# A first chunk prepared its own way: early statistics, own banks, and the spread of the deviations moved from memory to TensorE

## The chip, the cores and the metric

The kernel runs on one core of a Trainium2 chip. The time is that of the device, in microseconds, from the first to the last instruction of the core with what lies around them; lower is better. TensorE multiplies matrices into PSUM, ScalarE (ACT) and VectorE (DVE) work elementwise from PSUM and SBUF, GpSimd (POOL) elementwise from SBUF only, and SyncE (SP) issues the transfers here.

## The reference, cut to what matters

The input x is 32 images of 64 channels and 56 x 56 points, float32.

```python
x = x + conv_ref(ln_c(x))        # ln_c: mean and variance over the 64 channels of a point
t = to_tokens(x)                 # [32, 3136, 64]
t = t + ffn_ref(ln_t(t))         # ln_t: mean and variance over the 64 channels, eps 1e-5
x = from_tokens(t)

def conv_ref(x):                 # signs of the input, signs of the weights times a scale per channel
    y = conv3x3(sign(x), sign(w) * sw)
    y = (y - mean(y)) * rsqrt(var(y) + 1e-5) * gamma + beta   # mean, var over all images and points
    return clip(y, -1, 1)

def ffn_ref(x):                  # 8 experts of 64 hidden channels, weighted per token position
    feat = mean(x, axis=0)       # over the 32 images
    w = softmax(feat @ Wr + br)
    h = relu(bn1(x @ W1 + b1)); h = relu(bn2(h @ W2 + b2)); y = h @ Wo + bo
    return sum_over_experts(y * w)
```

The statistics of the convolution need all 32 images, so the second half can't begin before the convolution has ended.

## The kernel before, in words

**First stage, the convolution.** It goes over 16 pairs of images (TWOS) with four row groups each (GA). TensorE subtracts the channel mean (`centre_images`, L498) and convolves the signs, nine taps in bfloat16 (`conv_images`, L513). ScalarE takes the signs (L700) and keeps the sums y (L705). VectorE collects statistics of every kept group (`image_stats`, L852). The partitions hold 64 channels twice, once for the upper and once for the lower half of the image.

**Between the stages.** One `bn_aggr` (L872) makes mean and variance per partition from all 128 records of 6 values. TensorE averages the two halves with the matrix `halves` (L530), once for the mean and, after VectorE's corrections, once for the variance. ScalarE takes the root (L730), with a table load ahead of it and another behind it (L731). Six small VectorE steps (L885 to L895) make SCALE, OFFSET and OFFSET1.

**Second stage.** It goes over 28 chunks (RP). A chunk is one image row of each half, of all 32 images; it is cut into four groups of 8 images (G), 448 columns each (NG), and two steps p of two groups (STEPS). A chunk needs a preparation, `prep`, whose parts are:

- t: ScalarE, y times SCALE plus OFFSET1, clipped below (L762); x1: VectorE, clip above and add to x in place (L929)
- centre: TensorE subtracts the channel mean into banks 4 and 5 (Z of L2_BANKS) for step p (L601), ScalarE copies the deviations xc (L753); power: ScalarE squares xc into the tile `spread` (L757)
- var: TensorE sums the squares over the channels (L609) into bank Y; a group's variance lands in one row of the 32 rows of a quadrant. root, square, inv: inverse root rs with a Newton step (L765 to L772 ScalarE, L935 to L940 VectorE)
- spread_rs: SyncE writes the rows of rs to memory (four transfers, L287) and reads them back broadcast to all channels into `spread` (four transfers, L291); norm: GpSimd multiplies xc by spread (L422); feature: GpSimd sums over the images (L431 to L436)
- logits (L621), gate (softmax, L945 to L958 and L750), turn (transpose L628, placed L962, wT L776), wb (gate spread to the experts' channels L634 and L638, copied by L779 and L781)

The body of a chunk then runs eight units of six TensorE blocks: layer 1 (L545, two blocks, each followed by ScalarE's activation h, L738), layer 2 (L567, two blocks, each followed by VectorE's v, L908) and layer 3 (L583, two). A block is four matmuls, 64 rows by 64 columns of the array each, which the trace lists as eight instructions. `Schedule` STEADY gives the place among 96 half-unit points of the two chunks before it at which each part of a preparation is issued; AHEAD gives places for chunk 0, which has no chunk before it. Each engine works strictly in its own order, and waits are semaphores.

**The order before the first body.** On TensorE: all of chunk 0's preparation to the variance, the bias matmuls (L671, eight matmuls, needed for the constants `expert_const`), both layer-1 blocks of unit 0, the early part of chunk 1's preparation (`prep_early`), then chunk 0's logits, turn and wb. ScalarE, VectorE and GpSimd follow the same order. In chunk 0 the first and the second centring share banks 4 and 5, so that the second waits for the copy of the first:

```python
if at is AHEAD or isinstance(q, int) and q == 1:
    if q or p:
        pe.wait_ge(xc_kept, STEPS * q + p)
```

## Time and profile before

| | us |
|---|---|
| median of 3 runs | 1410.8 (1410.41 to 1419.26) |
| the profiled execution | 1413.79 |
| its span, first to last instruction | 1411.7 |
| TensorE busy in the span | 1326.0 (94%) |
| VectorE, ScalarE, GpSimd busy | 888.2, 868.5, 551.2 |

The busy share says how long an engine had an instruction in work; an idle engine costs time only where TensorE or the end waits for it. The chain that ended last tells this: it is followed back from the last instruction to whatever released each step. The granted clock is given as a share of 2.4 GHz. All times in rows count from the span's start, in one profiled execution.

### The profile page before, as it was taken

Reading aid. Unit: us, or ns where it says so; the run is one execution under the profiler, and the core shown is the slowest. Engines: PE = TensorE matmul, PEld = TensorE weight load, DVE = VectorE, ACT = ScalarE, POOL = GpSimd, SP = SyncE. Lnnn points to the kernel's source line nnn. Section 1 sums busy time; section 2 is a strip of 40 time slices with the busy share of each in tenths; the row PEclk is TensorE's granted clock in tenths of the full one; section 3 lists DMA queues with packets and bytes.
Section 4 is the critical chain, followed back from the end, with each engine's and each line's share of the span. In section 5 each row is a group of like instructions: output and inputs, shape, how many; then the busy total and the mean of one; then the engine's idle time right before and its main releaser. Section 6 shows DMA issues by size and latency. Waiting matters only on the chain.

```text
span 1411.7 us, 36466 instructions
## 1 busy us (share of the span) xinstructions
PE 1326.0 (94%) x14782; PEld 678.3 (48%) x14782; DVE 888.2 (63%) x1592; ACT 868.5 (62%) x1151; POOL 551.2 (39%) x474
## 2 busy tenths in 40 slices
PE   5798946999999999999999999999999999999998
PEld 3675732554444455445444444544454444444443
DVE  3343452666666767666666676667766677766655
ACT  4566654666666666666666666666666666666643
POOL 6104003444434444434444443444443444443441
PEclk9999966999999999999999999999999999999999
DMA  9977512233332323332233333233333232333121
GB/s 200 183 174 163 105 21 53 60 67 74 73 80 48 67 61 74 74 80 52 62 73 67 74 73 61 61 66 67 74 74 74 53 65 62 74 73 77 25 53 28
DMA packets 251026, 107.41 MB, mean 76 GB/s; under 512 B 238865, under 2 KB 239089, under 8 KB 250865
## 3 DMA queue, kind: packets, MB, share of 16 engines
q1 hardware_dynamic: 249600, 103.49, 34.9%
q8 instruction: 121, 1.98, 0.6%
q0 software_dynamic: 1264, 1.61, 0.6%
q14 instruction: 41, 0.33, 0.1%
HBM read 78.97 MB, written 26.09 MB: 74 GB/s over the span
## 4 chain that ended last, share of the span: by engine, by line
PE 92%; issue 3%; DMA 2%; DVE 1%; SPq 1%; ACT 1%; POOL 0%; POOLq 0%; DVEq 0%; ACTq 0%
PE ps L567 25%; PE ps L583 25%; PE ps L545 25%; PE ps L513 7%; PE ps L601 3%; PE ps L498 3%; PE ps L609 2%; PE ps L634 2%; DMA xa<-in_x 2%; PE ps L621 1%; PE ps L628 0%; SPq L266 0%; DMA spread<-rs_rows 0%; DVE bn L872 0%; ACT xc L753 0%
## 5 line engine op out<-in xcount | busy, mean ns | idle before, releaser
L908 DVE SCALAR_TENSOR_TENSOR v<-ps,negb,wb 128x448 f32<-128x448 f32 x896 | 571.0, 678 | 307.4 <-PE ps L567 306.2
L738 ACT ACTIVATE h<-ps,bias 128x896 f32<-128x896 f32 x448 | 451.5, 1008 | 332.1 <-PE ps L545 332.1
L545 PE MATMUL ps<-xc,w 64*64 64x448 f32 x3584 | 468.7, 542 | 15.2 <-POOL xc L422 11.3
L567 PE MATMUL ps<-h,w 64*64 64x448 f32 x3584 | 465.8, 541 | 5.6 <-issue 3.2
L583 PE MATMUL ps<-v,wo 64*64 64x448 f32 x3584 | 466.3, 539 | 3.7 <-issue 2.9
L583 PEld LDWEIGHTS ps<-v,wo 64*64 64x64 f32 x3584 | 179.1, 133 | 179.9 <-issue 160.6
L545 PEld LDWEIGHTS ps<-xc,w 64*64 64x64 f32 x3584 | 165.2, 132 | 189.6 <-issue 182.7
L567 PEld LDWEIGHTS ps<-h,w 64*64 64x64 f32 x3584 | 174.6, 133 | 161.9 <-issue 141.5
L452 POOL TENSOR_TENSOR o<-o,upper 128x448 f32<-128x448 f32 x112 | 127.3, 1137 | 299.8 <-DVE o L918 299.8
L444 POOL TENSOR_TENSOR o<-xin,gconst 128x448 f32<-128x448 f32 x112 | 130.6, 1186 | 235.9 <-ACT gconst L781 143.0
L422 POOL TENSOR_TENSOR xc<-xc,spread 128x896 f32<-128x896 f32 x56 | 123.5, 2221 | 209.9 <-DMA spread<-rs_rows 209.7
L513 PE MATMUL ps<-sgn,convw 64*64 64x392 bf16 x2304 | 124.4, 335 | 13.6 <-issue 12.8
L852 DVE BATCH_NORM_STATS2 stats<-y 128x6 f32<-128x392 f16 x128 | 66.4, 560 | 108.2 <-ACT y L705 108.2
L513 PEld LDWEIGHTS ps<-sgn,convw 64*64 64x64 bf16 x2304 | 92.4, 109 | 44.6 <-issue 25.9
L929 DVE SCALAR_TENSOR_TENSOR xin<-t,xin 128x448 f32<-128x448 f32 x112 | 96.6, 866 | 1.0 <-ACT t L762 0.9
L744 ACT ACTIVATE upper<-ps 128x448 f32<-128x448 f32 x112 | 60.6, 541 | 47.4 <-PE ps L583 47.4
L705 ACT ACTIVATE y<-ps 128x784 f16<-128x784 f32 x64 | 52.8, 825 | 57.2 <-PE ps L513 57.2
L762 ACT ACTIVATE t<-y,bn 128x448 f32<-128x448 f16 x112 | 83.3, 749 | 0.1
L918 DVE TENSOR_TENSOR o<-ps,o 128x448 f32<-128x448 f32 x112 | 69.0, 616 | 17.3 <-PE ps L583 17.3
L498 PE MATMUL ps<-xa,centre 64*64 64x392 f32 x512 | 71.0, 524 | 9.2 <-issue 5.8
L601 PE MATMUL ps<-xin,centre 64*64 64x448 f32 x448 | 64.9, 570 | 9.8 <-DVE xin L929 4.3
L753 ACT ACTIVATE xc<-ps 128x896 f32<-128x896 f32 x56 | 51.4, 918 | 36.2 <-PE ps L601 36.2
(143 smaller groups left out, 676.6 us busy)
## 6 DMA issues: line engine op xcount, KB each, us to landing
xa<-in_x SPq DMA_DIRECT2D x64, 392.0 KB, 7.4
xin<-in_x SPq DMA_DIRECT2D x112, 224.0 KB, 4.1
spread<-rs_rows SPq DMA_DIRECT2D x112, 224.0 KB, 4.1
out<-o SPq DMA_DIRECT2D x224, 112.0 KB, 2.5
rs_rows<-rs SPq DMA_DIRECT2D x112, 3.5 KB
rows<-in_L_ffn_g POOLq DMA_DIRECT2D x2, 256.0 KB, 12.9
rows<-in_L_ffn_v POOLq DMA_DIRECT2D x2, 256.0 KB, 14.8
cwt<-in_L_conv_weight SPq DMA_DIRECT2D x2, 144.0 KB, 2.7
```

The lines of the kernel that those rows point to most:

```text
L422: nc.gpsimd.tensor_tensor(xc[:, s, p], xc[:, s, p], spread[:, p], ALU.mult).then_inc(u_done[p], 1)
L444: nc.gpsimd.tensor_tensor(o[:, images, :], xin[:, s, images, :], gconst[:, s:s + 1, :].broadcast_to([P, BG, W]), ALU.add).then_inc(x1g_don ...
L452: nc.gpsimd.tensor_tensor(og, og, upper[:], ALU.add).then_inc(sum_done, 1)
L498: last = mm(ps[64 * high:64 * high + 64, A_BANKS[g % 2] + low, 0:NA], centre64[rows_, :], xa[rows_, xa_slot(m), low ^ high, g, :], start=T ...
L513: last = mm(ps[64 * high:64 * high + 64, CONV_BANKS[g % 2] + low, 0:NA], convw[rows_, tap, :], sgn[rows_, m % SRING, top:top + KG, kx:kx + ...
L545: last = mm(ps[64 * two:64 * two + 64, L1_BANKS + ab, 0:NG], w1[half, P * q + C * two:P * q + C * two + C], xc[half, s, g // 2, ab ^ (g % ...
L567: last = mm(ps[64 * i:64 * i + 64, L2_BANKS[ab] + low, 0:NG], w2[rows_, Q + QUADS * i, :], h[rows_, u % 2, i, ab, :], start=True, stop=True)
L583: last = mm(ps[64 * par:64 * par + 64, ACC_BANKS + low, 0:NG], wo[rows_, 2 * Q + d, :], v[rows_, u % 2, par ^ (g % 2), d, :], start=(Q == ...
L601: last = mm(ps[64 * high:64 * high + 64, Z + low, 0:NG], centre64[rows_, :], xin[rows_, s, BG * g:BG * g + BG, :], start=True, stop=True)
L738: A(h[:, u % 2, i], ps[:, L1_BANKS:L1_BANKS + 2, 0:NG], ACT.Relu, bias=bias[:, 0, q:q + 1]).then_inc(h_done[i], 1)
L908: last = V.scalar_tensor_tensor(out=v[:, u % 2, ab, d, :].rearrange("p (b w) -> p b w", w=W), in0=ps[:, L2_BANKS[ab] + d, 0:NG].rearrange( ...
L929: V.scalar_tensor_tensor(out=xg, in0=t[:, g].rearrange("p (b w) -> p b w", w=W), scalar=2.0, in1=xg, op0=ALU.min, op1=ALU.add).then_inc(x1 ...
```

## The change

- Statistics: after the fourteenth pair of images VectorE aggregates what there is (`old_stats`, 28 images, 672 of 768 values) and prepares products of the scales. After the last pair it aggregates the last four images (96 values), and weighs the two parts: the mean before the first matmul, the variance by two matmuls with `halves_old` and `halves_new` that add up. After the root three small steps remain.
- Chunk 0's centring goes to banks 4, 5 and 0, 1 (`FIRST_BANKS`), both steps without a wait between them. ScalarE squares straight from the banks, and VectorE copies xc.
- rs is spread by TensorE (`first_deviations`, eight matmuls with the selecting matrix `pick`) into banks 2 to 5, and VectorE multiplies xc by it from there; VectorE also does the sums over the images. SyncE, and GpSimd's norm and feature, have no part in chunk 0's preparation any more; waits that count on them (rs_kept, rb_loaded, p_feat) are lowered by one chunk.
- The order behind it: the bias matmuls and layer 1 follow the spread, and the parts of chunk 1's preparation are interleaved with chunk 0's logits, gate, turn and wb on each engine.
- At the start VectorE makes `halves_old`, `halves_new` and `pick`.

```diff
@@ constants on VectorE
+                V.tensor_scalar(halves_old[:], halves[:], 1.0 - NEW_SHARE, None, ALU.mult)
+                V.tensor_scalar(halves_new[:], halves[:], NEW_SHARE, None, ALU.mult)
+                row_of = [ident[:, C * p:C * p + C].rearrange("p (xy r o) -> p xy r o", xy=2, o=1)[:, :, 0:2, :].broadcast_to([P, 2, 2, C]) for p in range(STEPS)]
+                V.tensor_tensor(pick[:], row_of[0], row_of[1], ALU.add)
@@ statistics on VectorE (LATE = 2, NEW_SHARE = LATE / TWOS)
+                def old_stats():
+                    dve.wait_ge(a_stats, TWOS - LATE)
+                    step(V.bn_aggr(OLD, stats[:, 0:2 * (TWOS - LATE)].rearrange("p b g s -> p (b g s)")))
+                    step(V.tensor_scalar(OLD_MEAN, OLD[:, 0:1], 1.0 - NEW_SHARE, None, ALU.mult))
+                    dve.wait_ge(s_ffn, 16 * N_FFN)
+                    step(V.tensor_scalar(SW2, SW, SW, None, ALU.mult))
+                    step(V.tensor_scalar(SWG, SW, gb[:, 0:1], None, ALU.mult))
+                    step(V.tensor_scalar(BETA1, gb[:, 1:2], 1.0, None, ALU.add))
+
                 for m in range(TWOS):
                     for g in range(GA):
                         image_stats(m, g)
+                    if m == TWOS - LATE - 1:
+                        old_stats()
                 dve.wait_ge(a_stats, TWOS)
-                V.bn_aggr(bn[:, 4:6], stats[:].rearrange("p b g s -> p (b g s)")).then_inc(a_stats, 1)
+                step(V.bn_aggr(NEW, stats[:, 2 * (TWOS - LATE):].rearrange("p b g s -> p (b g s)")))
+                V.scalar_tensor_tensor(out=MEANS, in0=NEW[:, 0:1], scalar=NEW_SHARE, in1=OLD_MEAN, op0=ALU.mult, op1=ALU.add).then_inc(a_stats, 1)
                 dve.wait_ge(s_pe, 2)
+                step(V.tensor_copy(MEAN, ps[:, 0, 0:1]))
+                step(V.tensor_scalar(DEVS, bn[:, 18:22:2], MEAN, None, ALU.subtract))
+                for n, part in enumerate((OLD, NEW)):
+                    last = V.scalar_tensor_tensor(out=SQUARES[:, n:n + 1], in0=DEVS[:, n:n + 1], scalar=DEVS[:, n:n + 1], in1=part[:, 1:2],
+                                                  op0=ALU.mult, op1=ALU.add)
+                last.then_inc(a_stats, 1)
+                step(V.tensor_scalar(MINUS_MEAN, MEAN, -1.0, None, ALU.mult))
                 dve.wait_ge(s_pe, 3)
+                V.tensor_scalar(bn[:, 10:11], ps[:, 0, 1:2], SW2, BN1_EPS, ALU.mult, ALU.add).then_inc(a_stats, 1)
                 dve.wait_ge(s_act, 4)
+                step(V.reciprocal(bn[:, 15:16], bn[:, 11:12]))
+                step(V.tensor_scalar(SCALE, bn[:, 15:16], SWG, None, ALU.mult))
+                V.scalar_tensor_tensor(out=OFFSET1, in0=MINUS_MEAN, scalar=SCALE, in1=BETA1, op0=ALU.mult, op1=ALU.add).then_inc(s_bn, 1)
@@ statistics on TensorE
+                pe.wait_ge(a_stats, TWOS + 1)
+                mm(ps[:, 0, 0:1], halves[:], MEANS, start=True, stop=True).then_inc(s_pe, 1)
+                pe.wait_ge(a_stats, TWOS + 2)
+                mm(ps[:, 0, 1:2], halves_old[:], SQUARES[:, 0:1], start=True, stop=False)
+                mm(ps[:, 0, 1:2], halves_new[:], SQUARES[:, 1:2], start=False, stop=True).then_inc(s_pe, 1)
@@ before the first body, TensorE
-                prep_ahead(prep)
+                def first_centre(p):
+                    pe.wait_ge(x1_done, 2 * p + 2 + G)
+                    for low, high in TILES:
+                        rows_ = slice(64 * low, 64 * low + 64)
+                        g = 2 * p + (low ^ high)
+                        last = mm(ps[64 * high:64 * high + 64, FIRST_BANKS[p] + low, 0:NG], centre64[rows_, :],
+                                  xin[rows_, 0, BG * g:BG * g + BG, :], start=True, stop=True)
+                    last.then_inc(centre_done, 1)
+
+                def first_deviations():
+                    pe.wait_ge(rs_done, 1)
+                    pe.wait_ge(xc_kept, 1)
+                    for xy in range(2):
+                        for p, high in TILES:
+                            rows_ = slice(64 * p, 64 * p + 64)
+                            last = mm(ps[64 * high:64 * high + 64, L2_BANKS[xy] + p, 0:NG], pick[rows_, xy, high, :], rs[rows_, :],
+                                      start=True, stop=True)
+                    last.then_inc(first_spread, 1)
+
+                for p in range(STEPS):
+                    first_centre(p)
+                prep(AHEAD, 0, 0, AHEAD.var)
+                first_deviations()
...
-                prep_early(prep, 0, HALVES)
+                prep(AHEAD, 0, 0, AHEAD.logits)
+                prep(STEADY, 1, 1, STEADY.centre[0])
+                prep(AHEAD, 0, 0, AHEAD.turn)
                 pe.wait_ge(f_dve, 1)
-                prep(AHEAD, 0, 0, AHEAD.logits)
+                prep(AHEAD, 0, 0, AHEAD.wb)
+                prep(STEADY, 1, 1, STEADY.centre[1])
@@ before the first body, ScalarE
-                prep_ahead(prep)
-                prep_early(prep, 0, STEADY.centre[0])
+                prep(AHEAD, 0, 0, 0)
+                for p in range(STEPS):
+                    act.wait_ge(centre_done, p + 1)
+                    bank = FIRST_BANKS[p]
+                    A(spread[:, p], ps[:, bank:bank + 2, 0:NG], ACT.Square).then_inc(xc_done, 1)
+                prep(AHEAD, 0, 0, AHEAD.var)
+                for h_ in STEADY.t:
+                    prep(STEADY, 1, 1, h_)
                 for i in range(2):
                     layer1_out(0, 0, i)
-                prep_early(prep, STEADY.centre[0], HALVES)
-                prep(AHEAD, 0, 0, AHEAD.logits)
+                prep(AHEAD, 0, 0, AHEAD.gate)
+                prep(STEADY, 1, 1, STEADY.centre[0])
+                prep(STEADY, 1, 1, STEADY.power[0])
+                prep(AHEAD, 0, 0, AHEAD.turn)
+                prep(AHEAD, 0, 0, AHEAD.wb)
+                prep(STEADY, 1, 1, STEADY.centre[1])
+                prep(STEADY, 1, 1, STEADY.power[1])
@@ before the first body, VectorE
+                prep(AHEAD, 0, 0, 0)
+                for p in range(STEPS):
+                    dve.wait_ge(xc_done, p + 1)
+                    bank = FIRST_BANKS[p]
+                    V.tensor_copy(xc[:, 0, p], ps[:, bank:bank + 2, 0:NG]).then_inc(xc_kept, 1)
+                prep(AHEAD, 0, 0, AHEAD.var)
+                dve.wait_ge(first_spread, 1)
+                dve.wait_ge(xc_kept, STEPS)
+                for p in range(STEPS):
+                    V.tensor_tensor(xc[:, 0, p], xc[:, 0, p], ps[:, Y + p:Z + p + 1:Z - Y, 0:NG], ALU.mult).then_inc(u_done[p], 1)
+                for p in range(STEPS):
+                    dve.wait_ge(u_done[p], 2)
+                step(V.tensor_tensor(feat2[:], xc[:, 0, 0], xc[:, 0, 1], ALU.add))
+                for half in (NG // 2, NG // 4):
+                    step(V.tensor_tensor(feat2[:, :, 0:half], feat2[:, :, 0:half], feat2[:, :, half:2 * half], ALU.add))
+                V.tensor_tensor(feat[:], feat2[:, :, 0:W], feat2[:, :, W:2 * W], ALU.add).then_inc(feat_done, 1)
+                prep(STEADY, 1, 1, STEADY.x1[0])
+                prep(AHEAD, 0, 0, AHEAD.logits)
+                prep(STEADY, 1, 1, STEADY.x1[1])
+                prep(AHEAD, 0, 0, AHEAD.gate)
                 dve.wait_ge(s_pe, 4)
                 V.tensor_tensor(expert_const[0:2 * E, :], expert_const[0:2 * E, :], ps[0:2 * E, ACC_BANKS, 0:P], ALU.add).then_inc(f_dve, 1)
+                prep(STEADY, 1, 1, STEADY.x1[2])
+                prep(AHEAD, 0, 0, AHEAD.turn)
+                prep(STEADY, 1, 1, STEADY.x1[3])
@@ SyncE and GpSimd before the first body
-                spread_rs(0, 0)
-                for p in range(STEPS):
-                    norm(0, 0, p)
-                feature(0, 0)
```

## Rows read from the trace of the kernel before

**Rows 1.** Page: busy times, granted clock in 40 slices, chain that ended last
```profile
PE 1326.0 (94%) x14782; PEld 678.3 (48%) x14782; DVE 888.2 (63%) x1592; ACT 868.5 (62%) x1151; POOL 551.2 (39%) x474
...
PEclk9999966999999999999999999999999999999999
...
PE 92%; issue 3%; DMA 2%; DVE 1%; SPq 1%; ACT 1%; POOL 0%; POOLq 0%; DVEq 0%; ACTq 0%
```

**Rows 2.** Chain that ended last, in order of time: start us, us, what
```profile
193.96 0.17 DVE bn L895
...
208.16 0.64 DVE rs L940
...
211.54 4.04 DMA spread<-rs_rows
...
215.72 2.08 POOL xc L422
...
217.93 1.77 PE ps L545 x8
```

**Rows 3.** Windows (start:end us, length, busy times, granted clock, DMA), core 0
```profile
core 0: us, PE busy (x) PEld busy (x) DVE busy (x) ACT busy (x) POOL busy (x), PEclk, DMA share, GB/s
18.40:20.70 2.30, 0.00 (x0) 0.00 (x0) 0.00 (x0) 0.89 (x2) 2.30 (x5) 1.00 0.98 210
20.90:24.00 3.10, 3.10 (x32) 1.75 (x36) 0.00 (x0) 0.83 (x1) 3.10 (x6) 0.50 0.98 236
...
203.20:206.60 3.40, 3.40 (x24) 2.00 (x24) 0.00 (x0) 1.58 (x4) 0.00 (x0) 0.50 0.00 0
...
217.90:231.20 13.30, 7.53 (x42) 2.55 (x42) 1.76 (x8) 6.06 (x8) 6.20 (x5) 0.50 0.00 1
231.30:235.80 4.50, 4.50 (x24) 1.63 (x24) 0.00 (x0) 1.66 (x3) 2.01 (x2) 0.50 0.00 0
235.90:250.00 14.10, 13.69 (x144) 5.74 (x142) 9.68 (x17) 9.38 (x13) 2.65 (x4) 1.00 0.42 67
```

**Rows 4.** Timeline of the statistics' end: start us, us, engine, line, operation
```profile
186.50 3.62 DVE L872 BATCH_NORM_AGGREGATE bn<-stats 128x2 f32<-128x768 f32 x1
...
190.18 0.59 PE L530 MATMUL ps<-bn,halves 128*128 128x1 f32 x2 [5.64 <-DVE bn L872]
...
192.81 1.28 ACT L731 ACT_TABLE_LOAD   x1
...
194.15 2.06 ACT L762 ACTIVATE t<-y,bn 128x448 f32<-128x448 f16 x3
```

**Rows 5.** Timeline of VectorE late in the convolution stage
```profile
172.86 1.04 DVE L852 BATCH_NORM_STATS2 stats<-y 128x6 f32<-128x392 f16 x2 [1.13 <-ACT y L705]
```

**Rows 6.** Timeline of centring, square and variance of the first chunk
```profile
196.37 2.00 PE L601 MATMUL ps<-xin,centre 64*64 64x448 f32 x8 [4.32 <-DVE xin L929]
...
199.35 0.95 ACT L757 ACTIVATE spread<-xc 128x896 f32<-128x896 f32 x1
...
203.20 1.72 PE L609 MATMUL ps<-spread,var_ones 128*32 128x448 f32 x8 [2.01 <-ACT spread L757]
```

**Rows 7.** Timeline of a centring block at the high clock, and its copy
```profile
258.89 1.05 PE L601 MATMUL ps<-xin,centre 64*64 64x448 f32 x8
...
259.99 0.92 ACT L753 ACTIVATE xc<-ps 128x896 f32<-128x896 f32 x1 [0.47 <-PE ps L601]
```

**Rows 8.** Timeline from the bias matmuls to the body, low clock to high
```profile
204.70 1.91 PE L671 MATMUL ps<-wo,c2sel 128*16 128x64 f32 x16
...
219.76 1.01 ACT L738 ACTIVATE h<-ps,bias 128x896 f32<-128x896 f32 x1 [10.11 <-PE ps L545]
...
231.27 1.75 PE L634 MATMUL ps<-placed,to_half 64*64 64x448 f32 x4 [1.05 <-ACT wT L776]
...
235.90 0.98 PE L545 MATMUL ps<-xc,w 64*64 64x448 f32 x8
```

**Rows 9.** Instructions by line and shape, 185 to 250 us
```profile
L940 DVE TENSOR_TENSOR rs<-rs,sq 128x448 f32<-128x448 f32 x2 | 1.3, 626 | 0.1
```

More of the change, by code:

```diff
@@ L220, in metaformer_kernel @@
         AHEAD = Schedule(
[L221 to L222 removed]
+            t=(0, 0, 0, 0), x1=(0, 0, 0, 0), centre=(), power=(),
+            var=3, root=3, square=3, inv=(3, 3), logits=5, gate=6, turn=7, wb=8)
         def places_at(when, h):
@@ L237, in prep_point @@
                 prep(STEADY, k + 2, s, half)
-        def prep_ahead(prep):
-            for h in range(AHEAD.logits):
-                prep(AHEAD, 0, 0, h)
-        def prep_early(prep, first, end):
-            for h in range(first, end):
-                prep(STEADY, 1, 1, h)
         with nc.Block() as block:
```

62 lines of the change are left out of this document (21 added, 41 removed).

## The prediction

> **What bounds the kernel now.** I read the page first: TensorE is busy for 94% of the span, the chain that ended last runs through it for 92%, and its granted clock is full except around the fifth to seventh slice of forty [rows 1]. So removing work from another engine helps only where TensorE waits. The chain of waits in order of time shows the one long place where it does: between the last convolution (its output is copied out at 185.4) and the first full-pace block of layer 1 at 235.90. In that stretch everything hangs on one line of work: the statistics, the first chunk's deviations, their variance, its inverse root, then a round trip through memory that spreads it over the channels, then the product on GpSimd [rows 2]. After 235.9 TensorE works without gaps (13.69 of 14.1 us) at the high level of its clock, while in the stretch it ran at the low level, 1.2 GHz [rows 3]. The change touches only this stretch, so the prediction is the new time of that layer-1 block (unit 1, second half) against its old 235.90; every us gained there arrives at the end, since what follows is bound by TensorE and its order is kept.
>
> **Statistics.** Before, one aggregation over 768 values per partition takes 3.62 us, then two small matmul pairs and a train of tiny VectorE steps lead to the first normalised image group t at 194.15 [rows 4]. Now 672 of the values are aggregated two pair-steps earlier. Cost of that step: 3.62 x 672/768 = 3.2 us, plus four tiny steps, about 4.1 us on VectorE. It has cover: per image group VectorE works 1.04 us and idles 1.13 [rows 5], and of the eight groups still to come the first four have 4 x 1.13 = 4.5 us of idle, the others (at a pitch of 1.5 us) about 0.5 each. Without that cover it would cost up to 4 us at the end of the stage. What is left after the last group: aggregation of 96 values, by proportion 0.45 us, by proportion plus one tiny instruction (0.16) 0.6; I take 0.55. Then a step of 0.22, the means' matmuls 0.62 until read (0.59 of them busy), mean 0.16, deviations 0.21, two squares together 0.40, the variance matmuls, a step of 0.22, the root 0.20, and 0.03 to 0.06 between each. The second matmul step is now two matmuls (four instructions where there were two): between 0.62 as before and twice that, I take 1.12. After the root ScalarE loads a table, 1.28 us, and t started 0.06 after it [rows 4]. Behind the root VectorE had six tiny steps, the last of which ended at 194.13 [rows 2], 0.04 after the load; now it has three (reciprocal, scale, offset: 0.16, 0.21, 0.22), over 0.66 after the root. The three that are dropped gain nothing, for the load alone is the bound. Sum from the last statistics (186.47): 5.3 us, t at 191.8 instead of 194.15: **2.3 gained**. The Trainium skill (ScalarE: Activation LUTs, What ACT_TABLE_LOAD costs) puts a drain of about 1.38 us behind each load of a new set; by that the gain here would be 1.3 smaller. This case's trace does not agree: load and next activation start 1.34 apart, not 2.66.
>
> **Deviations and variance.** t, x1 and the first centring matmuls keep their order (2.2 us). Before, the second group of centring waited until ScalarE had copied the first out of its bank, and each group was copied (0.92) and then squared (0.95) in series [rows 6, 7]. Now both groups have banks: second group readable 1.5 + 1.83 + 0.2 = 3.5 us after the first starts (1.83 is the low-clock time from a block's start until ScalarE can read it [rows 8], 1.5 the pitch of a block, and the 0.2 is what the first group took more than others [rows 6]), squared from the bank in 0.95, and variance starts at 4.5 after the first instead of 203.20 - 196.37 = 6.83: **2.3 gained**, variance at 198.6. The VectorE copies (two of 896 elements, about 1.1 each) run beside it and end near 199.6, before VectorE is needed at 202.5. Variance to inverse root is unchanged, 5.6 us, so the root stands at 204.2 instead of 208.80 [rows 2].
>
> **Spread and product.** From there before: four writes, 1.3 us of landing, four reads landing in 4.04, GpSimd's product in 2.08, layer 1 at 217.93, together 9.1 us [rows 2]. Now: eight matmuls on TensorE. Four fill 1.5 us at the low clock, so these take 3.0 and are readable after 3.33. Product on VectorE of 128x896: the trace has 128x448 at 0.63 [rows 9]; twice that is 1.25, while ScalarE's copy of 896 is 0.92; I take 1.08, a column count doubled with the fixed part once. TensorE meanwhile runs the bias matmuls L671, which lay in a gap before and now stand behind the spread: 1.7 us [rows 8]. So TensorE is ready at 0.06 + 3.0 + 1.7 = 4.8 and the product at 4.5: layer 1 at 208.9, **4.35 gained**, 9.0 in all. SyncE's eight transfers and GpSimd's four instructions vanish; nothing waits behind them there.
>
> **Logits to the body.** Behind it, VectorE's line is the bound. Second product ready at 209.6; feature sums of 896, 448, 224 and 112 elements: 1.09 + 0.63 + 0.38 + 0.27 and gaps, done at 212.1 (GpSimd needed 2.07 for the first alone). Logits to TensorE and back 0.45, two tiny steps of 0.17, behind an x1 of the next chunk (0.62, as the trace's 0.63 for the same width): read at 213.15. Then the second x1 of chunk 1 until 213.8, which releases centring on TensorE; softmax goes on meanwhile (seven tiny steps and an exponential of 0.2, gate ready at 215.0, placed at 216.55). ScalarE is now the bound: centred group readable at 213.94 + 1.10 [rows 7], copy 0.92, square 0.95, transposed gate 0.21: 217.1. This order costs: the gate's copy stands behind copy and square of another chunk. Gate matmuls at 217.2, second centring behind them (0.85) at 218.05, readable 219.15, copy and square until 221.05, layer 1's activation 1.01 until 222.06, next block 222.2. Before, 4.6 us lay between the gate matmuls (231.27) and that block at 235.90 [rows 8], now 5.0, with the chunk-1 work inside it. Gained from layer 1 on: 18.0 - 13.3 = **4.7**. Sum 2.3 + 2.3 + 4.35 + 4.7 = **13.7 us**.
>
> **Which clock.** These last times use the high level of TensorE's clock: a block of eight instructions takes 0.76 us there (144 in 13.69) and 1.5 at the low level (24 in 4.5), and is readable after 1.10 instead of 1.83. Rows: the level rose between 20.9 and 24.2, after 3.1 to 3.3 us without a gap and at the end of the 4.5 us run from 231.3, and it did not rise in the run of 3.4 us from 203.2 [rows 3]. The new order makes one unbroken run from 204.2, of 3.0 + 1.7 + 1.5 = 6.2 us, longer than any run here after which the level had not risen. I therefore let it rise near 209; wherever in the second half of the run it rises, the sum moves by only 0.6. Whether it stays up is less sure: behind the run TensorE pauses 1.3, 1.4 and, with only the small transpose inside, 2.5 us, and after an idle 2.3 us from 18.4 the level was found low [rows 3]. I take that it holds, as the pauses are interrupted, and keep the fall as a rival.
>
> **The numbers.** The profiled execution took 1413.8 (span 1411.7 and 2.1 around it), 3.0 over the median of 1410.8. 1413.8 - 13.7 = 1400.1 for its like; against the median, 1410.8 - 13.7 = **1397.1 us**, or 0.97% less. A per cent, 14.1 us, is about what a measurement of this kernel can tell from no change, and the sum ends just beside it.
>
> **Rivals.** (a) The sum holds, the clock raised in the new run and kept: 0.50, own range 1395 to 1399.3 (matmul pair and aggregation at their bounds -0.6 to +0.3, five large VectorE steps at theirs -0.5 to +0.8, clock +-0.5, unseen gaps at semaphores up to +1). (b) The clock rises and falls again in the 2.5 us pause before the gate matmuls: these take 0.7 longer until the second centring starts (1.56 for 0.85), which is readable after 1.83 instead of 1.10. 1.4 less gained, 12.3, time 1398.5. For it: the 2.3 us at 18.4; against it: that pause was whole. Chance 0.28. (c) The clock stays low until the body, as before: layer 1's first activation +0.7, next block +0.7, centring +0.7, and then (b)'s 1.4, less 0.3 that other work covers. 3.2 less gained, 10.5, time 1400.3. For it speaks that from 217.9 to 231.2 a TensorE busy for 7.5 of 13.3 us stayed low; against it the length of the run. Chance 0.14. (d) Behind the table load, which is now the bound of its place, ScalarE is kept once more as long as the load took (1.28 [rows 4]), because nothing else hides it: gain 12.4, time 1398.4. Against it: t started 0.06 after the load; chance 0.03. This is what the rule of the Trainium skill on table loads, cited above, would do here; the trace does not bear it out. (e) Slower: the broken start leaves TensorE at the low level deep into the body. A block then takes 1.5 us instead of 0.75, so a unit of six blocks loses 4.5; the gain is gone after three units, and after six the time is 1410.8 - 13.7 + 27 = 1424. For it: the first units have gaps that wait for activations. Against it: the same gaps stood behind 235.9 before and the level held. Chance 0.03.
> The last 0.02 is for what I don't see. The likeliest is (a). Range: low end from (a) with its terms at their lower bounds and the earliest rise, 1394.5; high end (c) with 1 us of gaps, 1401.5. Faster by over 1% is under 1396.7: half of (a) and little else, 0.30. Slower 0.03, within 1% the rest, 0.67.
>
> **What would show it.** The profile after should have t at 191.8, right behind the table load; variance at 198.6 with no copy ahead of the second centring; 3.0 us of spread matmuls at 204.2 and no rs_rows transfer before the body; layer 1 at 208.9; granted clock rising between 207.6 and 211; ScalarE without gaps of note from 219.15 to the body; the block that stood at 235.90 at 222.2. Wrong would make it: statistics of the last images delayed by the early aggregation, a spread or product much longer than 3.3 and 1.1, a clock still at 0.50 at 215, or a first chunk whose units keep waiting for ScalarE.

## The result, and the profile after

The changed kernel took 1396.8 us in the median (4 runs, 1392.46 to 1398.97), the kernel before in the same comparison 1410.61 (4 runs, 1410.09 to 1419.26). The ratio is 0.9884 with a 95% interval of 0.9837 to 0.9931. A second comparison (after_again below) gave 0.9900 (0.9874 to 0.9925). The median that was forecast, 1397.1, was met within 0.3 us; but by the ratio the kernel became 1.0 to 1.2% faster, beyond the interval's reach of no change, and the forecast had given "within 1%" 0.67 and "faster" 0.30. Why the sum came out right and the chances did not is what follows: the forecast for the stretch before the body was 0.7 to 0.9 too large, since one of its terms was 1.0 to 2.1 too large and the others a little too small, and the time after it, for which nothing was forecast, can move by 3 us too.

The page of the changed kernel, TensorE's busy time and its granted clock in 40 slices: the sixth and seventh slice have 0.7 and 0.8 of the full clock, where [rows 1] had 0.6 twice. TensorE has 18 instructions more than before, 14800 for 14782. This number matters below.

```profile
PE 1319.1 (94%) x14800; PEld 656.1 (47%) x14800; DVE 902.8 (65%) x1607; ACT 866.8 (62%) x1149; POOL 539.5 (39%) x468
...
PEclk9999978999999999999999999999999999999999
```

The timeline of the changed kernel (start us, us, engine, line, operation, then idle time and what ended it), from the statistics to layer 1; it answers to [rows 4, 6]:

```profile
186.06 0.59 DVE L920 BATCH_NORM_AGGREGATE bn<-stats 128x2 f32<-128x96 f32 x1
...
186.89 0.38 PE L524 MATMUL ps<-bn,halves 128*128 128x1 f32 x2 [2.80 <-DVE bn L921]
...
189.46 1.28 ACT L754 ACT_TABLE_LOAD   x1
...
190.75 2.71 ACT L785 ACTIVATE t<-y,bn 128x448 f32<-128x448 f16 x4
...
192.87 3.27 PE L669 MATMUL ps<-xin,centre 64*64 64x448 f32 x16 [4.00 <-DVE xin L969]
...
196.21 0.92 ACT L826 ACTIVATE spread<-ps 128x896 f32<-128x896 f32 x1 [0.58 <-PE ps L669]
...
197.18 1.72 PE L608 MATMUL ps<-spread,var_ones 128*32 128x448 f32 x8 [1.04 <-ACT spread L826]
...
202.81 3.10 PE L680 MATMUL ps<-rs,pick 64*64 64x448 f32 x16 [3.92 <-DVE rs L980]
...
205.99 2.09 DVE L1030 TENSOR_TENSOR xc<-xc,ps 128x896 f32<-128x896 f32 x2 [3.23 <-PE ps L680]
...
207.22 0.98 PE L542 MATMUL ps<-xc,w 64*64 64x448 f32 x8 [0.31 <-DVE xc L1030]
```

The last four images are aggregated in 0.59 us, the table load ends at 190.74 and t starts at 190.75, both groups are centred in one run, VectorE's two products take 2.09, and layer 1 starts 4.47 after the inverse root (202.75) where it took 9.1 [rows 2]. The way on to the block that stood at 235.90 [rows 8]:

```profile
210.81 0.37 PE L618 MATMUL ps<-wr,feat 64*56 64x8 f32 x8 [0.46 <-DVE feat L1036]
...
212.27 1.65 PE L600 MATMUL ps<-xin,centre 64*64 64x448 f32 x8 [1.08 <-DVE xin L969]
...
214.92 0.95 ACT L780 ACTIVATE spread<-xc 128x896 f32<-128x896 f32 x1
...
216.22 1.76 PE L631 MATMUL ps<-placed,to_half 64*64 64x448 f32 x4 [2.19 <-ACT wT L799]
...
219.74 0.92 ACT L776 ACTIVATE xc<-ps 128x896 f32<-128x896 f32 x1 [1.07 <-PE ps L600]
...
222.63 0.98 PE L542 MATMUL ps<-xc,w 64*64 64x448 f32 x8
```

And its windows (columns as in [rows 3]):

```profile
core 0: us, PE busy (x) PEld busy (x) DVE busy (x) ACT busy (x) POOL busy (x), PEclk, DMA share, GB/s
...
202.80:205.50 2.70, 2.69 (x16) 0.80 (x16) 0.00 (x0) 0.82 (x2) 0.00 (x0) 0.50 0.00 0
205.80:212.30 6.50, 3.48 (x48) 1.74 (x45) 6.01 (x12) 2.01 (x2) 0.00 (x0) 1.00 0.00 0
212.60:222.00 9.40, 7.21 (x42) 3.11 (x34) 2.36 (x7) 4.90 (x9) 3.20 (x3) 0.50 0.00 1
223.00:237.00 14.00, 13.61 (x142) 6.00 (x136) 9.57 (x17) 9.53 (x14) 0.89 (x2) 1.00 0.37 63
```

The clock rose near 205.6, in the run that starts with the spread, and fell near 212.4, as the first centring of chunk 1 began and before the gate matmuls; it rose for good between 222.0 and 223.0. In the second trace of this kernel (after_again) it rose near 202.1, at the end of the bias matmuls, and fell near 208.9, behind that centring and again before the gate matmuls (210.03).

In the table, and from here on, the opening is the time from the last statistics record to the layer-1 block of unit 1 that stood at 235.90.

| from ... to | before | forecast | after | after_again |
|---|---|---|---|---|
| last record to t | 7.68 | 5.3 | 4.72 | 5.04 |
| t to variance | 9.05 | 6.8 | 6.43 | 6.43 |
| variance to inverse root | 5.59 | 5.6 | 5.57 | 5.58 |
| root to layer 1 | 9.14 | 4.7 | 4.47 | 5.07 |
| layer 1 to the block of unit 1 | 17.97 | 13.3 | 15.41 | 14.30 |
| sum | 49.43 | 35.7 | 36.60 | 36.42 |
| gained | | 13.7 | 12.8 | 13.0 |

The opening thus gave 12.8 to 13.0 us. The mean of the runs fell by 16.4 in the first comparison (9.7 to 23.0 by the interval of the ratio). In the second it fell by 15.7, while the ratio of 0.9900 stands for 14.1 (10.6 to 17.8). So 1 to 4 us seem to come from somewhere else, which is less than either interval can tell; the experiments below show it better.

### The profile page after: what moved, and what is told of

Read it like the earlier page. It is cut to its first block and busy times, and to the rows that moved or that the text cites. A ratio compares the mean times of both kernels' runs of the same rounds, so it can differ in the third digit from the quotient of the medians.

```text
span 1397.2 us, 36502 instructions
## 1 busy us (share of the span) xinstructions
PE 1319.1 (94%) x14800; PEld 656.1 (47%) x14800; DVE 902.8 (65%) x1607; ACT 866.8 (62%) x1149; POOL 539.5 (39%) x468
## 5 line engine op out<-in xcount | busy, mean ns | idle before, releaser
L564 PE MATMUL ps<-h,w 64*64 64x448 f32 x3584 | 455.5, 541 | 9.0 <-issue 6.7
L542 PE MATMUL ps<-xc,w 64*64 64x448 f32 x3584 | 457.6, 539 | 3.8 <-issue 3.2
L580 PE MATMUL ps<-v,wo 64*64 64x448 f32 x3584 | 454.8, 539 | 2.0 <-issue 1.2
L580 PEld LDWEIGHTS ps<-v,wo 64*64 64x64 f32 x3584 | 170.9, 133 | 184.3 <-issue 170.9
L564 PEld LDWEIGHTS ps<-h,w 64*64 64x64 f32 x3584 | 166.3, 133 | 169.3 <-issue 154.5
L542 PEld LDWEIGHTS ps<-xc,w 64*64 64x64 f32 x3584 | 161.4, 132 | 178.9 <-issue 174.2
L420 POOL TENSOR_TENSOR xc<-xc,spread 128x896 f32<-128x896 f32 x54 | 116.5, 2169 | 147.8 <-DMA spread<-rs_rows 147.5
L969 DVE SCALAR_TENSOR_TENSOR xin<-t,xin 128x448 f32<-128x448 f32 x112 | 104.6, 935 | 1.6 <-ACT t L785 1.5
L600 PE MATMUL ps<-xin,centre 64*64 64x448 f32 x432 | 59.2, 555 | 4.6 <-issue 3.4
## 6 DMA issues: line engine op xcount, KB each, us to landing
rows<-in_L_ffn_g POOLq DMA_DIRECT2D x2, 256.0 KB, 12.8
```

The lines of the kernel that those rows point to most:

```text
L420: nc.gpsimd.tensor_tensor(xc[:, s, p], xc[:, s, p], spread[:, p], ALU.mult).then_inc(u_done[p], 1)
L542: last = mm(ps[64 * two:64 * two + 64, L1_BANKS + ab, 0:NG], w1[half, P * q + C * two:P * q + C * two + C], xc[half, s, g // 2, ab ^ (g % ...
L564: last = mm(ps[64 * i:64 * i + 64, L2_BANKS[ab] + low, 0:NG], w2[rows_, Q + QUADS * i, :], h[rows_, u % 2, i, ab, :], start=True, stop=True)
L580: last = mm(ps[64 * par:64 * par + 64, ACC_BANKS + low, 0:NG], wo[rows_, 2 * Q + d, :], v[rows_, u % 2, par ^ (g % 2), d, :], start=(Q == ...
L600: last = mm(ps[64 * high:64 * high + 64, Z + low, 0:NG], centre64[rows_, :], xin[rows_, s, BG * g:BG * g + BG, :], start=True, stop=True)
L969: V.scalar_tensor_tensor(out=xg, in0=t[:, g].rearrange("p (b w) -> p b w", w=W), scalar=2.0, in1=xg, op0=ALU.min, op1=ALU.add).then_inc(x1 ...
```

## The experiments

The edits are shown shortened. Single runs scatter by several us (23 runs of the kernel before lay between 1403.1 and 1414.8), so the parts of the opening are read in the traces, and the ratio is used for sums.

### The changed kernel again

No edit.

> The changed kernel once more, to get its ratio with five rounds and a second trace of the opening. Theory A (the gain is what the opening of the second stage lost, 13.3 us from the last kept image group to the block of layer 1 that stood at 235.90): median 13 to 14 us under the kernel before, ratio 0.9900 to 0.9910, and single runs scatter by 3 to 6 us because short pauses in the 28 chunks differ from execution to execution. Rival C (the body of the chunks became faster too): more than 15 us, ratio under 0.9893, and the chunks after the first are shorter in the trace.

Measured: 0.9900 (0.9874 to 0.9925), mean 15.7 us less; opening 36.42, the table above. The convolution stage ended at 180.0 in this trace and at 186.0 in the first, which shows how much of a single run is not the opening. The ratio lies at the edge of theory A's range, the difference of the means lies in rival C's: the runs do not separate the two. In this trace the time from the block of unit 1 to the end is 1171.5 us, 4.3 less than before, in the first trace of the changed kernel 1174.6, 1.2 less.

### The statistics alone

```diff
+                    if m == TWOS - LATE - 1:
+                        old_stats()
+                step(V.bn_aggr(NEW, stats[:, 2 * (TWOS - LATE):].rearrange("p b g s -> p (b g s)")))
+                mm(ps[:, 0, 1:2], halves_old[:], SQUARES[:, 0:1], start=True, stop=False)
+                mm(ps[:, 0, 1:2], halves_new[:], SQUARES[:, 1:2], start=False, stop=True).then_inc(s_pe, 1)
```

> The kernel before with the statistics of the change alone (28 images aggregated ahead, three steps behind the root), everything else as before. Theory A: t starts 3.0 us earlier after the last kept group (4.7 instead of 7.7 us after the last record), the rest of the opening keeps its lengths, time 3.0 us less, ratio 0.998. Rival B (the clock decides the opening: what comes earlier is lost again while TensorE's level is low): t earlier by 3.0 but the block of unit 1 by less than 2. If the early aggregation had delayed the last records, t would gain under 1.

The timeline of this kernel, the table load behind the root and t:

```profile
190.36 1.28 ACT L739 ACT_TABLE_LOAD   x1
...
191.66 2.71 ACT L770 ACTIVATE t<-y,bn 128x448 f32<-128x448 f16 x4
```

t came 5.15 after the last record instead of 7.68: 2.5 gained, with the matmuls of the statistics at the low level (the first trace of the change had them at the high level and got 3.0). The opening was 45.60, 3.8 shorter: these 2.5, 0.8 between layer 1 and the gate matmuls, where in this execution the clock was high from 221.7, and 0.5 in small parts. Ratio 0.9999 (0.9980 to 1.0017), mean 1.1 less: the time did not show the 3.8. Theory A is right for the place, though 2.5 for its 3.0, and not for the total. This gap of 2.7 us stays open.

### Shared banks

```diff
-    for p in range(STEPS):
-        first_centre(p)                       # banks 4, 5 and 0, 1
+    for h_ in range(AHEAD.var):               # centre=(1, 2), power=(1, 2), both in banks 4 and 5
+        prep(AHEAD, 0, 0, h_)                 # ScalarE copies, then squares; no VectorE copy
```

> The changed kernel with the old centring: both steps through banks 4 and 5, each copied and then squared by ScalarE. Theory A: from t to the variance matmuls 9.0 us instead of 6.4, so 2.6 us more, time 2.6 above the changed kernel, ratio to before 0.992. Rival B: the shift moves the whole opening against the clock, the loss at the block of unit 1 lies anywhere from 1 to 4.

```profile
192.47 0.92 ACT L779 ACTIVATE xc<-ps 128x896 f32<-128x896 f32 x1 [1.66 <-PE ps L603]
...
193.48 1.77 PE L603 MATMUL ps<-xin,centre 64*64 64x448 f32 x8 [1.06 <-ACT xc L779]
...
196.26 0.95 ACT L783 ACTIVATE spread<-xc 128x896 f32<-128x896 f32 x1
...
197.26 1.72 PE L611 MATMUL ps<-spread,var_ones 128*32 128x448 f32 x8 [2.01 <-ACT spread L783]
```

t (188.10) to the variance took 9.16 instead of 6.43: 2.7, as theory A had it (2.6). The second centring again starts behind the copy, at 193.48. The ratio, 0.9886 (0.9854 to 0.9917), did not show the loss; six runs between 1385.5 and 1398.5 can't resolve it. The edit undoes two things at once, the own banks and the square taken straight from them with VectorE's copy beside it. Together they are worth 2.7 us in the opening, read in the trace, and not more than that is shown.

### Spread by memory

```diff
-                first_deviations()
-                    V.tensor_tensor(xc[:, 0, p], xc[:, 0, p], ps[:, Y + p:Z + p + 1:Z - Y, 0:NG], ALU.mult).then_inc(u_done[p], 1)
+                spread_rs(0, 0)
+                for p in range(STEPS):
+                    norm(0, 0, p)
+                feature(0, 0)
```

> The changed kernel with the spread through memory and the product and the sums over the images on GpSimd, as before; statistics, banks and the new order kept. Theory A: 9.1 us instead of 4.5 from the inverse root to layer 1, and the sums over the images end 6.5 instead of 3.4 us after layer 1 starts: together 7.7 us later, ratio to before 0.9955 (time 1404.5). Rival B (a large part of the spread's worth is the clock: the run of eight spread matmuls lifts it): the level stays low until the body and another 1 to 2 us are lost, 9 to 10 us, ratio 0.9965.

```profile
209.75 4.11 POOL L421 TENSOR_TENSOR xc<-xc,spread 128x896 f32<-128x896 f32 x2 [62.54 <-DMA spread<-rs_rows]
...
211.96 1.77 PE L546 MATMUL ps<-xc,w 64*64 64x448 f32 x8 [11.26 <-POOL xc L421]
...
213.99 2.07 POOL L430 TENSOR_TENSOR feat<-xc 128x896 f32<-128x896 f32 x1
```

Root to layer 1 took 9.08 (forecast 9.1) and layer 1 to the logits 6.69, for 4.47 and 3.59 in the changed kernel: the opening was 44.84, 8.2 longer. The clock stayed low until 229.2, as rival B had it: without the run of the spread TensorE did not get the high level. But the loss of 8.2 is nearer to theory A's 7.7 than to rival B's 9 to 10, so this part of the clock was worth some 0.5 us. Ratio 0.9978 (0.9960 to 0.9995), mean 2.7 less than before, while its opening was 4.6 shorter. Against the changed kernel the time lost 13 us where the opening lost 8.2. Again the totals differ by more than the openings, in the same direction as for the statistics alone.

### Idle matmuls in the pauses

```diff
     layer1(0, 0, 0, 0)
+    fill(1)                                   # mm(ps[:, 7, 0:NG], halves, rs), result unused
     layer1(0, 0, 0, 1)
     prep(AHEAD, 0, 0, AHEAD.logits)
+    fill(1)
     prep(STEADY, 1, 1, STEADY.centre[0])
     prep(AHEAD, 0, 0, AHEAD.turn)
+    fill(2)
```

> The changed kernel with four idle matmuls (128x128 by 448 columns, results unused) in TensorE's pauses: one between the two layer-1 blocks, one behind the logits, two behind the transpose. They compute nothing that is needed. Theory B (the fall of the granted clock at 212.5, in the pauses before the gate matmuls, cost the changed kernel 1.4 to 2 us of its forecast gain): the level stays high from about 206 on, the gate matmuls take 0.85 instead of 1.56 us until the next centring, and the block of unit 1 comes 1.4 to 2 us earlier. Theory A (the order of ScalarE's work is the bound whatever the clock): level high, block earlier by less than 0.5. If the idle matmuls only stand in the way: the block comes later by up to 1.5.

One window and three rows of this kernel:

```profile
207.20:220.70 13.50, 10.96 (x83) 4.35 (x80) 8.85 (x21) 7.62 (x11) 2.96 (x3) 1.00 0.00 1
```

```profile
213.99 1.77 PE L695 MATMUL ps<-rs,halves 128*128 128x448 f32 x4
215.95 0.97 PE L631 MATMUL ps<-placed,to_half 64*64 64x448 f32 x4 [0.18 <-issue]
...
220.74 0.98 PE L542 MATMUL ps<-xc,w 64*64 64x448 f32 x8 [1.45 <-issue]
```

Once up at 207.1 the level held. From the gate matmuls to the block it took 4.79 instead of 6.41, so **1.6 us was the price of the clock's fall** there, as theory B said, and this with four matmuls that compute nothing. From layer 1 (207.61) to the block it took 13.13, for the 13.3 that was forecast with a clock that holds. The opening was 33.48; what it gained ahead of layer 1 is partly another execution's clock, high from 196.8 to 200.2 as well. Ratio 0.9868 (0.9846 to 0.9890).

### Without the table loads

```diff
-    act.preload_act_table_set("sqrt_and_others"); ACT.Sqrt; load "natural_log_exp_and_others"
-    V.reciprocal(bn[:, 15:16], bn[:, 11:12])
+    A(bn[:, 11:12], bn[:, 10:11], ACT.Ln); A(bn[:, 15:16], bn[:, 11:12], ACT.Exp, scale=-0.5)
```

> The changed kernel without the two table loads around the root: the inverse root is made as exp(-0.5 ln v), both in the set that is loaded anyway, and VectorE's reciprocal falls away. Theory A (the load of 1.28 us is the bound between root and t): t starts right behind VectorE's two remaining steps, two activations (0.45) and 0.5 behind the variance instead of 0.20 + 1.28, so 0.5 us earlier; time 0.5 less, too little for the ratio, read in the trace. Rival: the load was covered and VectorE's steps are the bound: 0.0. Rival of the Trainium skill (ScalarE: Activation LUTs, What ACT_TABLE_LOAD costs), a drain of 1.38 us behind a load of a new set: t would come 1.9 earlier.

Here the clock had fallen at 185.0, before the statistics' matmuls, so t at 4.71 after the last record must be held against a trace with the load and nearly the same level: reordered, next, has 5.24. The clock drops out if the time is counted from the start of VectorE's last step before the root, behind which TensorE has no part: to t it is 1.77 us in both traces of the changed kernel, in stats_only, by_memory and reordered, and 1.23 in the three kernels without the load (no_load, reordered_no_load, kept_high). So the load was the bound, by 0.54 us over what stands behind it without a load. First the load and t of reordered, then the last activation and t of reordered_no_load (both edits together, below), which reads the same without a load:

```profile
189.32 1.28 ACT L754 ACT_TABLE_LOAD   x1
...
190.62 1.42 ACT L785 ACTIVATE t<-y,bn 128x448 f32<-128x448 f16 x2
```

```profile
183.53 0.20 ACT L754 ACTIVATE bn<-bn 128x1 f32<-128x1 f32 x1
...
184.28 2.72 ACT L785 ACTIVATE t<-y,bn 128x448 f32<-128x448 f16 x4 [0.54 <-DVE bn L934]
```

In no_load the two stand at 188.78 and 189.52, again 0.74 apart. In reordered t starts 0.02 after the load. A drain behind it would have shown here as 1.9 us instead of 0.5. Ratio 0.9866 (0.9843 to 0.9889), too wide to see half a us.

### Chunk 1's work in idle places

```diff
     # TensorE
     layer1(0, 0, 0, 0)
+    prep(STEADY, 1, 1, STEADY.centre[0])
     layer1(0, 0, 0, 1)
     prep(AHEAD, 0, 0, AHEAD.logits)
-    prep(STEADY, 1, 1, STEADY.centre[0])
+    prep(STEADY, 1, 1, STEADY.centre[1])
     prep(AHEAD, 0, 0, AHEAD.turn)
     pe.wait_ge(f_dve, 1)
     prep(AHEAD, 0, 0, AHEAD.wb)
-    prep(STEADY, 1, 1, STEADY.centre[1])
     # VectorE: all four x1 of chunk 1 before dve.wait_ge(first_spread, 1)
     # ScalarE: h, copy 0, h, gate, copy 1, transposed gate, square 0, square 1, gate copies
```

> The changed kernel with chunk 1's share placed where engines are idle: VectorE makes its four x1 while TensorE spreads, TensorE centres step 0 between the two layer-1 blocks and step 1 behind the logits, ScalarE copies each at once, and squares both behind the transposed gate while the gate matmuls run. Theory A (from layer 1 to the body the bound is ScalarE's and VectorE's order, in which chunk-1 work stands ahead of chunk 0's gate): gate matmuls 1.5 to 2 us earlier, no centring behind them, the block of unit 1 3.5 us earlier than in the changed kernel, ratio to before 0.988. Theory B (the clock is the bound): less than 2.

```profile
207.70 0.93 PE L600 MATMUL ps<-xin,centre 64*64 64x448 f32 x8
...
213.74 1.76 PE L631 MATMUL ps<-placed,to_half 64*64 64x448 f32 x4 [1.21 <-ACT wT L799]
```

Opening 33.00, 3.4 to 3.6 shorter than the changed kernel's (forecast 3.5). The first centring of chunk 1 runs between the two layer-1 blocks, and from gate matmuls to the block it is 4.64 instead of 6.41, at the low clock. The order of ScalarE and VectorE was a bound, as theory A said; the clock was one too, as the idle matmuls showed. Ratio 0.9859 (0.9834 to 0.9885).

### Both edits

> Both edits together, reordered and without the table loads. Theory A: the two gains add, 4.0 us under the changed kernel, about 17.5 under the kernel before, ratio 0.9875. If the two share a bound: no more than the larger alone.

Opening 31.86, 4.6 to 4.7 under the changed kernel, of which 0.5 is the load's. It is 1.1 under reordered, 0.6 more than the load explains; the statistics' matmuls ran at the high level here and at the low one there. Ratio 0.9857 (0.9828 to 0.9886), mean 20.1 us less, as much as reordered alone. The gains add in the trace; the time, with both 1383.5 and 1395.7 among six runs, cannot show it.

### The kernel before again, and padded

The kernels so far fall into two families. Where TensorE spreads, the mean time gained 2.6 to 6.3 us more than the opening; where memory spreads, 1.8 and 2.7 less. The 28 chunks, untouched by any edit, were the place to look. Theory D: they differ by where TensorE's instructions lie in its stream.

```diff
     # before_padded: the kernel before, ahead of its first layer1, where TensorE waits 11 us
+    for _ in range(9):
+        mm(ps[:, 7, 0:8], halves[:], halves[:, 0:8], start=True, stop=True)
     # after_padded: the changed kernel, ahead of first_deviations, 16 of them
```

> The kernel before itself, for a second trace of it and as a zero for the comparison. All theories: ratio 1.000 +- 0.002, the opening from the last record to the block of unit 1 again 49.4 within 1. Theory A takes the 28 chunks' length of the first trace (1175.8 us from that block to the end) as typical; theory D (below) too; if it is 1171 or less here, the difference between the families of kernels is scatter.

> The kernel before with 9 tiny matmuls (8 columns, 18 instructions, results unused) ahead of its first layer-1 block, where TensorE waits 11 us anyway. The changed kernel has 18 instructions more on TensorE than the kernel before. Theory D (the short pauses in the chunks hang on where TensorE's instructions lie in its stream, and the changed kernel's chunks are 4 us shorter in sum because its stream is shifted): the chunk lengths take the changed kernel's pattern (long fourteenth, short fifteenth, last 40.4 instead of 42.0), block to end 1171, ratio 0.9965 to 0.9975. Theory A or plain scatter: pattern of the kernel before, ratio 1.000 +- 0.002.

> The changed kernel with 16 such matmuls (32 instructions) while TensorE waits 4 us for the inverse root. Theory D: the chunk lengths follow neither of the two patterns seen, and the sum may lie up to 5 us to either side of the changed kernel. Theory A: same pattern and ratio as the changed kernel, 0.990.

The last full chunk, from its gate matmuls to the next chunk's: the kernel before, the padded one, the changed one.

```profile
1323.67 0.95 PE L634 MATMUL ps<-placed,to_half 64*64 64x448 f32 x4
...
1365.67 0.95 PE L634 MATMUL ps<-placed,to_half 64*64 64x448 f32 x4
```

```profile
1318.22 0.95 PE L634 MATMUL ps<-placed,to_half 64*64 64x448 f32 x4
...
1358.60 0.95 PE L634 MATMUL ps<-placed,to_half 64*64 64x448 f32 x4
```

```profile
1310.90 0.95 PE L631 MATMUL ps<-placed,to_half 64*64 64x448 f32 x4
...
1351.27 0.95 PE L631 MATMUL ps<-placed,to_half 64*64 64x448 f32 x4
```

It is 42.00 us in the kernel before, 40.38 in the padded one and 40.37 in the changed one. The table has the row of 26 chunk lengths (between the starts of the gate matmuls, from the second on) and the time from the block of unit 1 to the end of the span:

| kernel | TensorE instructions | last chunk | 26 chunks | block to end | correlation of the 26 lengths with after_again |
|---|---|---|---|---|---|
| before | 14782 | 42.00 | 1092.0 | 1175.8 | 0.21 |
| before_again | 14782 | 41.73 | 1091.4 | 1175.9 | 0.29 |
| stats_only | 14784 | 41.89 | 1090.5 | 1174.5 | 0.13 |
| by_memory | 14784 | 41.56 | 1091.5 | 1175.9 | 0.07 |
| before_padded | 14800 | 40.38 | 1088.6 | 1171.1 | 0.75 |
| after | 14800 | 40.37 | 1091.3 | 1174.6 | 0.78 |
| after_again | 14800 | 40.39 | 1088.7 | 1171.5 | itself |
| no_load | 14800 | 40.39 | 1088.5 | 1171.9 | 0.81 |
| reordered | 14800 | 40.38 | 1086.2 | 1169.8 | 0.84 |
| reordered_no_load | 14800 | 40.38 | 1085.7 | 1169.7 | 0.74 |
| shared_banks | 14800 | 40.35 | 1082.6 | 1166.0 | 0.60 |
| filled | 14808 | 41.12 | 1085.3 | 1169.2 | 0.61 |
| after_padded | 14832 | 41.28 | 1085.4 | 1170.2 | 0.08 |
| kept_high, below | 14914 | 42.12 | 1087.0 | 1170.3 | -0.14 |

With 18 instructions more and nothing else, the kernel before moves over to the changed kernel's side. Its last chunk is 40.38, and from the block to the end it takes 1171.1, as theory D forecast; the kernel before has 1175.8 and again 1175.9, so that this is not scatter of one trace. Its 26 lengths correlate with the two traces of the changed kernel at 0.63 and 0.75, with those of its own kind at 0.34 and 0.41. The long fourteenth and the short fifteenth chunk of theory D did not come: 42.6 and 41.9 us, for 44.2 and 40.7 in the changed kernel. The ratio is **0.9973 (0.9959 to 0.9988)**, mean 3.4 us less, and the opening 49.11 for 49.43. The untouched copy had 1.0010 (0.9995 to 1.0026). The granted clock was 1.00 from 260 to 1360 us in all fourteen traces, so the clock is not what differs. The other padded kernel follows neither pattern and has 0.9877 (0.9854 to 0.9900) with an opening of 37.89, from which nothing more follows: theory D had allowed 5 us to either side.

So it is shown that the place of the instructions in TensorE's stream alone can be worth 3.4 us (1.7 to 5.8 by the interval). That the changed kernel's 1 to 4 us are this is argued, from the same number of instructions and a like pattern; its two traces have only 1.2 and 4.3 us less from the block to the end. What makes the place count, the loading of the instructions for instance, is not shown. In the last chunk the kernel before has two pauses of TensorE that the trace puts down to issue (no cause that the profile shows), of 1.1 and 0.6 us, and the padded kernel has none; but between 236 and 1380 us these pauses add up to 11.2 us in both.

### The level kept high

```diff
     # reordered_no_load with 57 of these, 3 to 16 in each of TensorE's waits before the body
+    def fill(bank, n):
+        for _ in range(n):
+            mm(ps[:, bank, 0:P], halves[:], halves[:], start=True, stop=True)
```

> The reordered kernel without table loads, with 57 idle matmuls (128 columns, 0.21 us each at the high level) in TensorE's waits from the end of the convolution to the body, so that the level never falls. Theory B (the level costs what the rows say: 1.5 for 0.76 a block, 1.83 for 1.10 until readable): centring to variance 3.0 instead of 4.3, root to layer 1 2.9 instead of 4.9, gate matmuls to the block 3.0 instead of 4.6, from the last record to the block 27 instead of 31.9; ratio to before 0.9825 to 0.984. Theory A: ScalarE and VectorE bound these stretches, gain under 1.5, ratio 0.985. If idle matmuls do not hold the level: no change, or later by the ones in the way.

```profile
181.60:209.80 28.20, 25.52 (x228) 16.06 (x226) 16.91 (x38) 16.96 (x27) 0.98 (x1) 1.00 0.00 1
```

```profile
189.10 0.98 PE L675 MATMUL ps<-xin,centre 64*64 64x448 f32 x8 [0.33 <-DVE xin L979]
...
199.43 0.98 PE L548 MATMUL ps<-xc,w 64*64 64x448 f32 x8 [0.50 <-DVE xc L1042]
...
206.77 0.97 PE L637 MATMUL ps<-placed,to_half 64*64 64x448 f32 x4
...
209.80 0.98 PE L548 MATMUL ps<-xc,w 64*64 64x448 f32 x8
```

The level was high throughout (1.00 from 181.6 to 209.8, TensorE busy for 25.5 of 28.2 us, 12.0 of them with idle work). Gate matmuls to the block: 3.03, forecast 3.0. First centring to variance: 3.5 (forecast 3.0), root to layer 1 3.28 (2.9); in both, TensorE now waits for VectorE, at 189.10 for x1 and at 199.43 for the product. Opening 28.23, forecast 27, and 3.6 less than the same kernel without idle matmuls, where theory A allowed 1.5. Ratio **0.9811 (0.9786 to 0.9836)**, median 1385.4 against 1411.8: the fastest version here, 0.7 to 0.9% ahead of the changed kernel, whose intervals begin at 0.9837 and 0.9874; those of reordered and reordered_no_load overlap with this one's. The opening is 21.2 us shorter than before, the mean time 26.7. The ratio is better than theory B's 0.9825 to 0.984 too; this kernel has its own place in the stream (14914 instructions), and what it owes to that is open.

## Why the prediction was right and wrong, step by step

**Statistics**, forecast 2.3, measured 3.0 and 2.6 in two traces. The early aggregation hid as forecast (3.19 us at 171.32, caught up by 178.9), the last one took 0.59 for 0.55. The table load was the bound behind the root, as no_load shows. Mis-sized were the means' matmuls, taken as 0.62 until read and 0.42 in both traces, and in the first trace the second matmul step, taken as 1.12 and 0.80 there; in the second trace it was 1.12. The short values go with the high clock, which had not yet fallen when the matmuls came so early (it fell at 188.5 in the first trace; in the second at 181.6, between the two steps).

**Centring**, forecast 2.3, measured 2.6; shared_banks, which undoes it, lost 2.7. **Spread and product**, forecast 4.35, measured 4.7 and 4.1. VectorE's product of 128x896 from a bank took 1.08, as was chosen between 0.92 and 1.25. The clock rose in the run, 2.8 us after its start in the first trace, earlier than the forecast's window, and 5.0 after it in the second, where the bias matmuls took 1.9 instead of 1.1; this makes the 0.6 between the two.

**Layer 1 to the block**, forecast 4.7, measured 2.6 and 3.7. The step that failed here was "I take that it holds, as the pauses are interrupted". The level fell at 212.4 in the first trace, as chunk 1's centring began and so before the pause that rival (b) named, and at 208.9 in the second, in that pause; (b), given 0.28, is what happened, not (a). From the gate matmuls to the block it took 6.41 in both traces for the forecast 5.0, which is (b)'s 1.4; filled gave 1.6 back and with the level held met the forecast of the whole place, 13.13 for 13.3. The 0.7 more of the first trace lies in the centring that ran low, 1.65 for 0.98. That the copy of the gate stands behind chunk-1 work is a cost too: reordered took 2.8 to 3.9 out of this place.

**The body**, forecast nothing, measured 1.2 and 4.3 us in the traces. The sentence "every us gained there arrives at the end, since what follows is bound by TensorE and its order is kept" was the one that failed most: it put the body's own change at nothing. The order was kept, but 18 instructions were added before it, and before_padded shows that this alone is worth 3.4 us (1.7 to 5.8 by the interval). That the median was met within 0.3 us is luck: an opening 0.8 short of its forecast, an unpriced gain behind it and the runs' scatter cancelled. By the means the kernel gained 16.4 and 15.7, by the second ratio 14.1.

**The chances.** "A per cent, 14.1 us, is about what a measurement of this kernel can tell from no change" did not hold either: the first interval reaches 0.47% to either side, the second 0.26%. With a forecast beside the bound of 1%, an unpriced term of 1 to 4 us was enough to turn the likelier side; the chance of 0.30 for faster was too small. The own range of (a) is also added up wrongly: its terms, -1.6 to +2.6, give 1395.5 to 1399.7, not 1395 to 1399.3. The total range, 1394.5 to 1401.5, holds the median all the same.

**Rivals.** (c), a clock low until the body, fell: it rose in the run of the spread, which by_memory, without that run, did not have. (d), a ScalarE kept busy behind the table load, fell: t started 0.01 after it. The Trainium skill (ScalarE: Activation LUTs, What ACT_TABLE_LOAD costs) puts a drain of about 1.38 us behind the load at every switch of sets; no trace here agrees, as t started 0.01 to 0.07 us after the load wherever there was one. (e), a low clock deep into the body, fell: the level was 1.00 from 223.0 on.

**Open.** stats_only and by_memory were 2.7 and 1.8 us slower than their openings say against the kernel before. Both have 14784 instructions, two more than it, and nearly its pattern of chunks; whether the two instructions cost this or the scatter did is not settled.

## What to carry to other kernels

Where one engine is the bound of the long part, price the short serial part by its chain, but look also at what the clock does in it: matmuls that compute nothing, put in TensorE's waits, brought 1.6 us with four and, with 57 of them, took 3.6 us out of the opening of the fastest version here. Work for a later stage belongs where its engine waits anyway, not ahead of a small step that others wait for. And before a difference of 0.3% in a stage that no edit touched is explained, add a few idle instructions to the old kernel: here that moved it by as much.

## What the runs showed of the hardware

- The lengths of 26 equal chunks of TensorE work (40.3 to 44.2 us) repeat from trace to trace as long as TensorE's instruction count is the same or nearly so: any two of the seven traces with 14800 instructions correlate at 0.50 to 0.87, any two of the four with 14782 or 14784 at 0.65 to 0.89, one of either kind with one of the other at 0.07 to 0.53.
- Tiny matmuls with 18 instructions, placed in a wait of 11 us, made the 1176 us behind them 4.7 us shorter in the trace, at the same granted clock.
- The granted clock fell near 212.4 us although no pause of TensorE was longer than 1.2 us in the 6.5 us before (busy 3.48 of 6.5), and it stayed up when four matmuls raised this to 10.96 of 13.5.
- An aggregation of 672 values per partition took 3.19 us, of 768 3.62 and of 96 0.59, so 0.0045 us a value and 0.16.
